# A gated cross-attention and FFN block: one stage's weight jobs turned in two ways, a second output bank, preparation reordered

## The reference

```python
x = x + tanh(g_xattn) * xattn(layernorm(x), ctx)      # 16 heads of 64, ctx has 64 rows per batch, causal mask
x = x + tanh(g_ffn)   * ffn(layernorm(x))

def ffn(x):                                           # w_gate, w_up: 1536 x 512, w_down: 512 x 1536
    x = act_qdq(x)                                    # 16-bit: scale = max|x| / 32767 over the WHOLE tensor
    up, gate = act_qdq(x @ dq(w_up).T), act_qdq(x @ dq(w_gate).T)
    gate = act_qdq(gate * fixed_qdq_u16(sigmoid(gate)))
    return act_qdq(gate * up) @ dq(w_down).T
# dq(w): 4-bit in blocks of 32 of a row: s = max|block| / 7; clip(round(w / s)) * s
```

## Time and profile before

| | us |
|---|---|
| median of three runs (1363.0 to 1367.02) | 1364.11 |
| the profiled execution | 1361.4 |
| its span, first to last instruction | 1359.2 |
| front, the opening to 68 us and the steps to 493 us | 493 |
| gate stage | 503 to 763 |
| up stage, a stretch without matmuls, down stage | 768 to 1359 |

### The profile page before, as it was taken

How to read it: one execution, slowest core, us unless ns; L and a number is a source line. 1 busy time by engine, 2 the same in 40 slices (tenths; PEclk the granted TensorE clock), 3 DMA queues, 4 the chain that set the end, 5 groups by cost and what they waited for, 6 DMA issues and landing times. The chain is left out here.

```text
span 1359.2 us, 18938 instructions
## 1 busy us (share of the span) xinstructions
PE 1229.2 (90%) x5985; PEld 600.9 (44%) x5985; DVE 1002.8 (74%) x1444; ACT 672.7 (49%) x782; POOL 285.8 (21%) x375
## 2 busy tenths in 40 slices
PE   7889999999899989999999999999990079999998
PEld 6644534544454444444444444444440034444443
DVE  2678778778777667777776599979999974545544
ACT  3444444444444234444443488857769964334341
POOL 0145426525633322111111122201110000000000
PEclk9999999999999999999999999999995589999999
DMA  9113423523433456677774799953378853445453
GB/s 335 28 40 102 139 78 93 143 73 93 130 94 109 132 176 224 218 249 216 245 203 155 266 317 339 345 180 135 136 264 322 318 188 136 158 169 178 155 175 110
DMA packets 174346, 243.48 MB, mean 179 GB/s; under 512 B 86224, under 2 KB 98512, under 8 KB 174288
## 3 DMA queue, kind: packets, MB, share of 16 engines
q1 hardware_dynamic: 174000, 242.80, 54.5%
q10 hardware_dynamic: 288, 0.00, 0.0%
HBM read 136.32 MB, written 91.23 MB: 167 GB/s over the span
## 5 line engine op out<-in xcount | busy, mean ns | idle before, releaser
L1903 PE MATMUL pD<-Wh,xph 128*128 128x512 f16 x384 | 145.5, 379 | 1.0 <-DVE xpl L1878 1.0
L1380 PE MATMUL gpG<-xph,Wh 128*128 128x512 f16 x384 | 145.8, 380 | 0.2 <-DVE xpl L1302 0.2
L1380 PE MATMUL gpG<-xpl,Wh 128*128 128x512 f16 x384 | 145.8, 380 | 0.0
L1380 PE MATMUL gpG<-xph,Wl 128*128 128x512 f16 x384 | 145.8, 380 | 0.0
L1380 PE MATMUL pU<-xph,Wh 128*128 128x512 f16 x384 | 145.5, 379 | 0.0
L1380 PE MATMUL pU<-xpl,Wh 128*128 128x512 f16 x384 | 145.5, 379 | 0.0
L1380 PE MATMUL pU<-xph,Wl 128*128 128x512 f16 x384 | 145.5, 379 | 0.0
L1903 PE MATMUL pD<-Wl,xph 128*128 128x512 f16 x384 | 145.5, 379 | 0.0
L1903 PE MATMUL pD<-Wh,xpl 128*128 128x512 f16 x384 | 145.5, 379 | 0.0
L1285 ACT ACTIVATE gst<-gpG,rw 128x512 f32<-128x512 f32 x96 | 65.8, 686 | 148.1 <-PE gpG L1380 144.5
L1041 PE MATMUL pO<-Vh,pTh 128*128 128x512 f16 x256 | 97.9, 383 | 15.3 <-DVE x L824 13.0
(11 more groups left out here) (239 smaller groups left out, 2461.5 us busy)
## 6 DMA issues: line engine op xcount, KB each, us to landing
dub<-up_d SPq DMA_DIRECT2D x42, 768.0 KB, 4.7
gate_d<-gst SPq DMA_DIRECT2D x96, 256.0 KB, 2.5
gb<-gate_d SPq DMA_DIRECT2D x24, 768.0 KB, 6.7
up_d<-ust SPq DMA_DIRECT2D x72, 256.0 KB, 4.7
eu<-up_d SPq DMA_DIRECT2D x22, 768.0 KB, 6.1
xr<-xn_d SPq DMA_DIRECT2D x9, 1024.0 KB, 6.4
xin<-in_x SPq DMA_DIRECT2D x32, 256.0 KB, 3.5
x_d<-x SPq DMA_DIRECT2D x32, 256.0 KB, 2.3
```

Source lines behind the costliest of these rows:

```text
L1380: mm = pe.matmul(ps[:, :], Ws[:, it, kt * P:(kt + 1) * P], xs[:, kt, :], start=(kt == 0 and Ws is Wh and xs is xh), stop=(kt == KT - 1 and ...
L1903: mm = pe.matmul(pD[4 * t + q][:, :], os_[n][:, cs], Ws[:, it, :], start=(it == 0 and os_ is oh and Ws is Wh), stop=(it == IT - 1 and os_ ...
```

## The change

The front gets a second output bank: tile j's output goes to pO or pX by j % 2, and TensorE waits for the residual of tile j-2 in place of j-1. In the opening, w_o's maximum moves ahead of fit_a, and in step 0 the statistics of tile 2 move ahead of the maximum over the values. In the V step VectorE does two low parts ahead of the sums, not one.

In the gate stage w_up's jobs (t = 0) are no longer turned by TensorE. ScalarE's high and VectorE's low part are made from the rows in SBUF (d); at it = 5, 9, 11 SP waits for the low part and turns both with transposing transfers into new buffers; at (t, it) = (0, 8), (0, 11) and (1, 2) it waits for these and stores them. w_down's jobs stay as they were, with their counts halved.

```diff
+        pOut = [pO, pX]
 def residual(b, j):
-                dve.scalar_tensor_tensor(out=x1[n][:, :], in0=pO[:, :], scalar=O_SCALE, in1=xin[j % BQ][:, :],
+                dve.scalar_tensor_tensor(out=x1[n][:, :], in0=pOut[n][:, :], scalar=O_SCALE, in1=xin[j % BQ][:, :],
 def normal():
-                    if have(k + 2) and k + 2 >= 2:
+                    if have(k + 2) and k + 2 > 2:
                         statistics(b, k + 2)
                 if k == 0:
+                    statistics(b, 2)
                     dve.wait_ge(v_sb, ROUNDS)
                     largest_of(3, flat(vT))
...
                 if which is not None:
-                    some(2 if which == 0 else 1)
+                    some(2)
                 if have(k - 1):
                     sums(b, k - 1)
...
+            dve.wait_ge(wo_in, 16)
+            largest_of(2, flat(wo))
             dve.wait_ge(id_set, 2)
             fit_a()
-            dve.wait_ge(wo_in, 16)
-            largest_of(2, flat(wo))
             schedule(dve, step, straight=True)
 def values(b, k, have):
-                    pe.wait_ge(*tile(x1_done, b, j - 1))
+                    pe.wait_ge(*tile(x1_done, b, j - 2))
-                            mm = pe.matmul(pO[:, :], ps_[:, cs], vs[:, p, :],
+                            mm = pe.matmul(pOut[j % 2][:, :], ps_[:, cs], vs[:, p, :],
 gate_phase:
+        turned = [[sb(ph, f"gj{part}T{n}", [P, 512], F16) for part in ("hi", "lo")] for n in range(3)]
+        turn_in = [sem(f"gj_turn_in{n}", 32) for n in range(3)]
 def traffic(sp, i, last=False):
+                    if (t, it) in ((0, 8), (0, 11), (1, 2)):
+                        q = ((0, 8), (0, 11), (1, 2)).index((t, it))
+                        dsts = job_dst(i, q)
+                        sp.wait_ge(*at(turn_in[q], 32 * i, 32))
+                        sp.sem_inc(J.apart, 1)
+                        for part, dst in zip(turned[q], dsts):
+                            sp.dma_start(dst, part[:, :]).then_inc(J.stored[q], 16)
                     if it in (5, 9, 11):
                         q = 3 * t + (5, 9, 11).index(it)
-                        job_store(sp, J, i, q, job_dst(i, q))
+                        if t:
+                            job_store(sp, J, i, q, job_dst(i, q))
+                        else:
+                            sp.wait_ge(*at(J.lo_done, JR * i, q + 1))
+                            sp.sem_inc(J.apart, 1)
+                            sp.wait_ge(*at(J.stored[q], 32 * i, 0))
+                            sp.sem_inc(J.apart, 1)
+                            for part, to in zip((J.hi[q], J.lo[q]), turned[q]):
+                                sp.dma_start_transpose(to[:, :].rearrange("p (k n) -> p k n", n=P), part[:, :]).then_inc(turn_in[q], 16)
 def evictions(i, last=False):
-                            job_hi(act, J, i, 3 * t + it // 4)
+                            q = 3 * t + it // 4
+                            if t:
+                                act.wait_ge(*at(J.stored[q], 32 * i, 0))
+                                act.wait_ge(*at(J.turned, 3 * i, q - 2))
+                                act.activation(J.hi[q][:, :], J.bank[0][:, :], ACT.Copy).then_inc(J.hi_done, 1)
+                            else:
+                                act.wait_ge(*at(J.deq_done, JR * i, q + 1))
+                                act.wait_ge(*at(turn_in[q], 32 * i, 0))
+                                act.activation(J.hi[q][:, :], J.d[q][:, :], ACT.Copy).then_inc(J.hi_done, 1)
 def extremes(i, last=False):
-                            job_integer(dve, J, i, q, (10 * i, 5 * t + 5))
+                            dve.wait_ge(*at(J.row_done, 10 * i, 5 * t + 5))
+                            dve.wait_ge(*at(J.int_done, JR * i, q + 1))
+                            dve.wait_ge(*at(J.lo_done, JR * i, q - 5))
+                            dve.tensor_tensor(blocks(J.d[q][:, :]), blocks(J.q[q][:, :]), spread(J.sn[:, q, :]), ALU.mult).then_inc(J.deq_done, 1)
-                        if it % 4 == 3:
+                        if it % 4 == 3 and t:
                             job_lo(dve, J, i, q)
+                        if it % 4 == 3 and not t:
+                            dve.wait_ge(*at(J.hi_done, JR * i, q + 1))
+                            dve.wait_ge(*at(turn_in[q], 32 * i, 0))
+                            dve.tensor_tensor(J.lo[q][:, :], J.d[q][:, :], J.hi[q][:, :], ALU.subtract).then_inc(J.lo_done, 1)
 def gates(i, last=False):
-                        if it % 4 == 3:
+                        if it % 4 == 3 and t:
                             job_turn(pe, J, i, 3 * t + it // 4, ident)
```

## The result

The changed kernel takes 1345.4 us (median of 4 runs, 1344.4 to 1350.1) against 1365.4 us of the kernel before in the same runs (1363.0 to 1367.0): ratio 0.9861, 95% interval 0.9843 to 0.9879. Forecast were 1348.3 us from 1364.1. The profiled execution took 1344.4 us against 1361.4; on this pair the sum was made, and it says 17.0 where 15.8 were forecast. In the fences, the number after L is the changed kernel's line.

What follows compares the result with a forecast made beforehand. TensorE was taken to bound the gate stage, with neither TensorE nor VectorE full in the front. Opening 5.4, V 1.0 + 2.4, bank 1.8 and gate stage 5.2 sum to 15.8 us off: 1364.1 to 1348.3 us, range 1342 to 1356.

Steps and rivals of the forecast that it cites:

- Opening, 5.4: Opening: with both moves the scores start at about 51.0 us, not 56.36, and the half-speed stretch goes; 5.4 us off.
- Three V steps, 0.8 each: Three later V steps: TensorE no longer waits for the second low part; 0.8 us each, 2.4 us off.
- V's part in the opening, 1.0: The opening's V step: of its 2.8 us wait for low parts about 1.0 us is gained.
- Bank, 1.8: Front: the second output bank gains only the wait right after V is made, three times 0.6 us: 1.8 us off.
- The main statement: w_gate steps: waits for the residual turn into a longer wait for pr, grown by some 8 to 10 us; gain zero.
- Gate stage, 5.2: Gate stage: twelve of 24 jobs lose their TensorE transposes, 0.44 us each; 5.2 us off.
- cost 0: Gate stage: added waits and transfers on SP delay tile stores, but the stage buffers' slack covers it; cost 0.
- Rival E: Gate stage: transposes hold SP's queue until TensorE stalls; slower, 1372 us at 7 us a transfer; chance 0.05.
- The clock: Half-speed stretches in the w_gate steps: neither an end nor new ones counted, 0; ends 1.4 us gained, 3.5 lost.
- Rival C: Front: one more 3.4 us half-speed stretch heading each of three key steps; 9.2 us off, 1355 us; chance 0.08.

Runs made afterwards that it cites:

- e2: The kernel before with the two moves of the opening alone (w_o's maximum, statistics of tile 2): ratio 0.9945.
- e7: The kernel before with 16 idle matmuls on TensorE inside its 4.3 us wait of the opening: ratio 0.9976.
- e4: The kernel before with two of V's low parts ahead of the sums, alone: ratio 0.9973.
- e1: The kernel before with the second output bank alone: ratio 0.9982.
- e3: The kernel before with the new gate stage alone: ratio 0.9953.
- e9: The changed kernel with w_up's transposing transfers issued twice, the first pair into spare tiles: 1360.8 us in one execution.
- e10: The changed kernel with five of six jobs turned by transfers, w_down's third by TensorE: median 1344.5 us, ratio 0.9856 to the kernel before.
- e11: The changed kernel with GpSimd making pr ahead of the w_gate job's low part: 1347.6 us, ratio 0.9869 to the kernel before.
- e12: e10 with filling matmuls in TensorE's waits (8 and 6 in the opening's V step, 10 in each of three key steps): 1342.0 us, ratio 0.9839 to the kernel before.

## Why the prediction was right, and which steps were not

- **Opening, 5.4: measured 5.1.** The order of the links was as worked out: w_o landed at 31.87 (31.7 forecast), xn at 44.54 (44.9), keys resume at 46.77 (47.1) after 0.45 us of idle time (0.4), the slow stretch there went, the scores start at 50.66, or 51.2 with the earlier start taken off (51.0). From the first keys matmul the gain is 5.2, in after and in e2 alike. e7 showed that filling the idle time is enough to make the stretch go, with the order of the work unchanged.
- **Three V steps, 0.8 each: 0.84 each,** in after and in e4.
- **V's part in the opening, 1.0: 0.2. This step failed.** I split a wait of 2.8 us by judgement, without writing down which low part comes when. The third group of V waits for the first two low parts, the fourth for four. In after the sums stand between the first two and the next two:

```profile
62.98 1.41 DVE L783 SCALAR_TENSOR_TENSOR Vl<-pT,fit,Vh 128x512 f16<-128x512 f32 x2 [3.19 <-ACT Vh L699]
64.30 1.21 DVE L839 TENSOR_REDUCE ssum<-pr 128x16 f32<-128x1024 f32 x1
65.55 0.25 DVE L842 RECIPROCAL srec<-ssum 128x16 f32<-128x16 f32 x1
65.72 1.32 DVE L783 SCALAR_TENSOR_TENSOR Vl<-pS,fit,Vh 128x512 f16<-128x512 f32 x2
```

  So the third group is released earlier and the fourth is now the one behind the sums: the one wait of 2.8 us became two, 1.5 and 1.6. The wait was moved on, not taken away.
- **Bank, 1.8: about 1.5.** 0.64 and 0.80 where no slow stretch disturbs the pair, some 0.6 from tiles 10 to 16 once a stretch's 1.4 us (below) is taken from the 2.02, and 0.5 lost from tiles 2 to 8, which I had not forecast and e1 shows as well (87.61 with one slow stretch, against 85.68). The 0.5 is what VectorE's wait for the w_gate job's load grew by there, from 2.81 to 3.30 us (3.43 in e1); that the one makes the other is read from the traces, no run changed it. The main statement held: the 13.0 us turned into a wait for pr, from 2.5 us in 8 waits to 15.6 in 10. Its reason was incomplete: VectorE's chain in these steps is not only work, it holds the three waits for a job's load (8.4 us before, 8.9 in after).
- **Gate stage, 5.2: 5.1** (5.5 from its first matmul), in e3 4.3 with a slow stretch in it. Product by product the twelve turned jobs' pitch fell from 3.03 to 2.59 us, which is the 0.44 of the sum. No wait for a store reached TensorE, and the three tile stores of the earlier trace rows start 104.9 us after the stage's third matmul (105.2 before), with two transposes now ahead of them. But the cover grew thin, which "cost 0" did not say: ScalarE's 38.8 us of waits for DMA (24.7 + 14.1) were 2.2 before, and a store of gate's tiles landed after 3.2 us and not 2.5. The Trainium skill, "VectorE: DVE Perf Modes", section "The three transpose paths", has 1309 ns for a 128x128 block by DMA, four times which is 5.2 us, an estimate by that page. The rows above have four such blocks issued in 1.20 us and landed after 2.5 us, so the trace does not agree with that estimate.
- **Rival E was priced too cheaply.** I let the delay be free up to 6 us and put the even point at 6 us a transfer. e9 adds 2.5 us a pair, well under that, and loses 13.0 us, 4.2 to 4.5 in each of three rounds. The mistake: I looked at one turn of the queue, where 1 us of slack stood before ScalarE, and took the PSUM banks as a fresh reserve at each. In truth three pairs come within six tiles, some 16 us, with x's own four transposes (5.41 us of the queue, at 602.57 in after) right behind, and e9 loses only in the halves where these follow. The forecast stood on the safe side of that edge by less than it said.
- **The clock was left out of the sum, and is probably the rest.** I counted 0 for new or vanished stretches outside the opening. Tiles 10 to 16 take 86.25 us without a slow stretch (after) and 87.6 to 87.8 with one (e10, e11): 1.4 us each. The profiled kernel before has four in the front and its end, the changed one one. Over all executions the kernel before took 1360.6 us at a mean clock of 0.969 (one execution), 1362.9 at 0.966 (22), 1364.8 at 0.965 (14) and 1367.3 at 0.962 (8), with 13 more in between; the changed one 1344.4 to 1345.6 at 0.969 (three) and 1350.1 at 0.965. At equal mean clock the change is worth 15.6 (0.969) and 14.7 (0.965), which is close to the forecast's sum; the rest of the 20 us would be that three in four of its executions ran at the higher mean. A mean doesn't say where the stretches lie, so this split is a reading of the times and not shown by a run of its own. Rival C had the right cause, and the sign wrong: fewer stretches, not more. In single executions (1350.1 here, 1350.9 in e10) something of it is seen.

## What to carry to other kernels

A wait's total is a gain only if the engine has no other wait behind it: read who is late next, and expect the same microseconds under another name. Where two pieces of work stand ahead of one late instruction, moving one alone can be worth nothing and both the whole. A queue that is free for nearly a third of a stage can have no room left where its long transfers come close together; measure its edge by issuing them twice, and look at where the loss lies before you divide it by their number. A wait for another engine can end in a load further back: follow it until an engine or a queue is found that was working.

## What the runs showed of the hardware

A transposing transfer of 128x512 16-bit elements holds SP's queue for 1.20 to 1.26 us against 0.33 to 0.53 for a plain one (medians of the gate stage, after), and lands after 2.5 us (median) in after and 2.5 to 2.7 in e9, at DMA shares of 0.78 and 0.82. e9's 24 more of them left the landing of plain stores at 3.2 us and made others wait in the queue. A half-speed stretch of 3.4 us followed TensorE's wait of 4.2 to 4.3 us in the opening in five traces of five, and none followed there in the nine traces with 2.1 us or less; elsewhere such stretches follow some idle times and not others (a wait of 3.29 us at 144 us was followed by none in after), and they come at other places in other executions. 16 filling matmuls inside one idle time (e7), or 44 in five of them (e12), took slow stretches away, and the work behind came no more than 0.2 us later in any of the table's stretches of the front (e12 against after).
